# Window attention's norm roots: Newton rounds on VectorE replaced by ScalarE's Ln and Exp with one Newton round

## The reference

```python
def l2norm(t):
    return t / jnp.maximum(jnp.linalg.norm(t, axis=-1, keepdims=True), 1e-12)
...
qkv = x @ Wqkv
q, k, v = jnp.split(qkv, 3, -1)
...
q = l2norm(q) * qs
k = l2norm(k) * ksc
q = q * cos * scale + rotate_half(q) * sin * scale
k = k * cos * inv + rotate_half(k) * sin * inv
out = local_attention(q, k, v)      # softmax over 64 keys per query
```

## Time and profile before

| | |
|---|---|
| median of 3 runs | 5156.09 us (5155.09 to 5167.56) |
| the profiled execution | 5172.85 us |
| its span in the trace | 5170.8 us |
| TensorE matmul, weight load busy | 76%, 56% of the span |
| VectorE (DVE) busy | 4374.4 us, 85% |
| ScalarE (ACT) busy | 3040.4 us, 59% |
| GpSimd (POOL) busy | 2537.9 us, 49% |

### The profile page before, as it was taken

One profiled execution on the slowest core, in us unless ns is written; L12 is line 12 of the kernel. 1 busy time (PEld: TensorE's weight loads), 2 busy tenths in 40 slices (PEclk: granted clock), 3 DMA queues, 4 the chain that ended last, 5 costly groups with the idle time before them and its releaser, 6 DMA issues. The chain is left out here.

```text
span 5170.8 us, 110439 instructions
## 1 busy us (share of the span) xinstructions
PE 3934.8 (76%) x39280; PEld 2903.7 (56%) x39280; DVE 4374.4 (85%) x7725; ACT 3040.4 (59%) x4888; POOL 2537.9 (49%) x1612
## 2 busy tenths in 40 slices
PE   5777777777777777767858678777787787777787
PEld 4655655656656646625535466466465565565565
DVE  8988989979979979954335399799799899898897
ACT  4765756746747747722413477477476476575575
POOL 5645646636636636611010266366366365464562
PEclk8988999989989989986978899899899998899899
DMA  1000000000000000021030000000000000000000
GB/s 47 8 23 11 7 22 12 8 27 6 7 27 7 8 25 8 8 62 26 2 74 1 33 7 7 26 8 21 13 8 20 14 8 19 15 7 22 12 7 12
DMA packets 30608, 88.57 MB, mean 17 GB/s; under 512 B 7505, under 2 KB 13649, under 8 KB 28369
## 3 DMA queue, kind: packets, MB, share of 16 engines
q1 hardware_dynamic: 29104, 80.95, 5.9%
q10 hardware_dynamic: 1152, 3.15, 0.2%
HBM read 38.72 MB, written 1.05 MB: 8 GB/s over the span
## 5 line engine op out<-in xcount | busy, mean ns | idle before, releaser
L771 POOL TENSOR_TENSOR pool<-pool 128x512 f32<-128x512 f32 x768 | 1069.1, 1413 | 968.3 <-DVE pool L869 968.3
L776 POOL TENSOR_TENSOR pool<-pool 128x1024 f32<-128x1024 f32 x384 | 1072.8, 2794 | 168.0 <-DVE pool L880 147.2
L443 PE MATMUL psum<-squares,pool 128*128 128x128 f32 x3072 | 475.4, 304 | 420.8 <-POOL pool L776 259.9
L443 PEld LDWEIGHTS psum<-squares,pool 128*128 128x128 f32 x3072 | 368.9, 153 | 587.2 <-issue 338.1
L880 DVE TENSOR_TENSOR pool<-pool 128x1024 f32<-128x1024 f32 x384 | 678.6, 1806 | 6.8
L483 PE MATMUL psum<-wqkv_hi,xs_lo 128*128 128x512 f32 x1152 | 522.2, 453 | 200.3 <-DVE pool L849 104.6
L646 ACT COPY pool<-psum 64x512 f32<-64x512 f32 x768 | 447.1, 582 | 367.1 <-PE psum L443 361.7
L474 PE MATMUL psum<-pool 128*64 128x128 f32 x6144 | 560.7, 296 | 116.7 <-ACT pool L661 116.5
L420 PE MATMUL psum<-pool 128*128 128x128 f32 x3072 | 455.4, 309 | 130.2 <-ACT pool L646 129.8
L859 DVE TENSOR_REDUCE pool<-pool 128x16 f32<-128x1024 f32 x384 | 449.9, 1210 | 88.1 <-ACT pool L685 88.0
L420 PEld LDWEIGHTS psum<-pool 128*128 128x128 f32 x3072 | 420.4, 219 | 179.4 <-ACT pool L646 167.8
(11 more groups left out here) (165 smaller groups left out, 8247.6 us busy)
## 6 DMA issues: line engine op xcount, KB each, us to landing
pool<-pool SPq DMA_DIRECT2D x192, 128.0 KB, 2.3
pool<-in_wqkv SPq DMA_DIRECT2D x12, 1536.0 KB, 6.0
k_st<-turn_st SPq DMA_DIRECT2D x8, 1536.0 KB, 21.3
pool<-in_wo SPq DMA_DIRECT2D x12, 512.0 KB, 3.6
pool<-in_w SPq DMA_DIRECT2D x12, 341.0 KB, 3.0
pool<-in_w SPq DMA_DIRECT2D x12, 192.0 KB, 2.9
rotary<-in_rotary SPq DMA_DIRECT2D x2, 1024.0 KB, 5.4
pool<-in_scale SPq DMA_DIRECT2D x12, 128.0 KB, 6.2
```

The source lines that it names most:

```text
L443: last = pe.transpose(bank(7 - p % 2)[:, P * j:P * j + P], rot[:, p // 2, 2 * c:2 * c + 2, :], ident)
L771: last = g.tensor_tensor(rot[:, q, :, hd * r:hd * r + hd], qn[:, q, :, hd * (1 - r):hd * (2 - r)], tab, ALU.mult)
L776: g.tensor_tensor(rot[:, q], rot[:, q], by_cos[:, q], ALU.add).then_inc(rot_ready, 1)
```

## The change

A tile `least` of 128x32 is set to 1e-24 once. VectorE's `rsqrt` for the norms goes. In its place VectorE takes the maximum of the sums of squares and `least` into `held`; ScalarE, behind the softmax exponent of U-2 and ahead of `take`, computes `logs = Ln(held)` and `root = Exp(-0.5 logs)`; VectorE executes all softmax pieces of U-2 in a row, waits for `root_ready` and does one Newton round of three operations into `norm`. The other users of `rsqrt` (the layer norms) stay.

```diff
--- before.py
+++ after.py
@@ -45,6 +45,7 @@
         band_b = sb("band_b", [P, NT, 2 * WIN], bf16)
         ones = sb("ones", [P, P])
         mean_w = sb("mean_w", [P, P])
+        least = sb("least", [P, 2 * HEADS])
         ln_a = sb("ln_a", [P, B * NT])
         ln_s = [sb(f"ln_s{i}", [P, B * NT]) for i in range(4)]
 
@@ -64,6 +65,8 @@
         k_kept, s_ready, s_taken, p_ready = sem("k_kept"), sem("s_ready"), sem("s_taken"), sem("p_ready")
         block_ready, pt_ready = sem("block_ready"), sem("pt_ready")
         o_ready, o_out, wo_ready, y_ready = sem("o_ready"), sem("o_out"), sem("wo_ready"), sem("y_ready")
+        ss_ready, ss_held = sem("ss_ready"), sem("ss_held")
+        log_ready, root_ready = sem("log_ready"), sem("root_ready")
         norm_step, soft_step = sem("norm_step"), sem("soft_step")
 
         mu_ready, xc_ready, fsq_ready, var_ready = sem("mu_ready"), sem("xc_ready"), sem("fsq_ready"), sem("var_ready")
@@ -93,8 +96,8 @@
         counted = {
             "tensor": [qk_ready, v_ready, t_ready, s_ready, o_ready, wo_ready, mu_ready, var_ready,
                        rb_ready, w1_ready, w2_ready],
-            "scalar": [xs_ready, sq_ready, v_out, t_out, p_ready, pt_ready, o_out, fsq_ready, gel_ready],
-            "vector": [qn_ready, cos_ready, s_taken, block_ready, y_ready, norm_step, soft_step,
+            "scalar": [log_ready, root_ready, xs_ready, sq_ready, v_out, t_out, p_ready, pt_ready, o_out, fsq_ready, gel_ready],
+            "vector": [ss_ready, ss_held, qn_ready, cos_ready, s_taken, block_ready, y_ready, norm_step, soft_step,
                        xc_ready, diag_ready, xn_ready, hid_ready, x_ready, var_step, aff_step],
             "gpsimd": [lo_ready, w_hi, w_split, sin_ready, rot_ready, turn_ready, k_kept],
         }
@@ -176,6 +179,7 @@
                 v.tensor_copy(band_b[:].rearrange("p t k -> p (t k)"),
                               mask_f[:]).then_inc(set_up, 1)
                 v.memset(ones[:], 1.0)
+                v.memset(least[:], 1e-24)
                 v.memset(mean_w[:], 1.0 / D).then_inc(set_up, 1)
 
             @block.scalar
@@ -270,7 +274,7 @@
             by_cos = cut(2, HEADS, DH)
             rot = cut(2, HEADS, DH)
             ss = cut(2 * HEADS)
-            nwt = [cut(2 * HEADS) for _ in range(4)]
+            held, logs, root, newt, norm = [cut(2 * HEADS) for _ in range(5)]
             qT = cut(PAIRS, P)
 
             kT = [cut(PAIRS, 2, WIN + P) for _ in range(2)]
@@ -665,6 +669,13 @@
                             a.wait_ge(s_taken, done(U))
                             a.activation(S, S, ACT.Exp).then_inc(p_ready, 1)
 
+                        def roots(U):
+
+                            a.wait_ge(ss_held, done(U))
+                            a.activation(logs, held, ACT.Ln).then_inc(log_ready, 1)
+                            a.wait_ge(log_ready, done(U))
+                            a.activation(root, logs, ACT.Exp, scale=-0.5).then_inc(root_ready, 1)
+
                         def products(U):
 
                             a.wait_ge(o_ready, done(U))
@@ -686,6 +697,8 @@
                                                  ACT.Square).then_inc(sq_ready, 1)
                             if has(2):
                                 exponents(U0 + 4 * i + k - 2)
+                            if has(0):
+                                roots(U)
                             if has(-1):
                                 take(i, k + 1)
                             if has(3):
@@ -859,15 +872,24 @@
                                     last = v.tensor_reduce(ss[:, HEADS * q:HEADS * (q + 1)],
                                                            sq[:, INNER * q:INNER * (q + 1)].rearrange(
                                                                "p (h e) -> p h e", e=DH), AX.X, ALU.add)
-                                last.then_inc(norm_step, 1)
-                                v.wait_ge(norm_step, done(U, RSQRT + 1, 0))
-                                rsqrt(v, ss, nwt, norm_step, done(U, RSQRT + 1, 0), ALU.max, 1e-24, None, None,
-                                      between=probabilities(U - 2) if has(2) else ())
+                                last.then_inc(ss_ready, 1)
+                                v.wait_ge(ss_ready, done(U))
+                                v.tensor_tensor(held, ss, least[:], ALU.max).then_inc(ss_held, 1)
+                                if has(2):
+                                    for piece in probabilities(U - 2):
+                                        piece()
+                                v.wait_ge(root_ready, done(U))
+                                v.scalar_tensor_tensor(newt, root, -0.5, held, ALU.mult, ALU.mult).then_inc(norm_step, 1)
+                                v.wait_ge(norm_step, done(U, 3, 0))
+                                v.tensor_tensor(newt, newt, root, ALU.mult).then_inc(norm_step, 1)
+                                v.wait_ge(norm_step, done(U, 3, 1))
+                                v.scalar_tensor_tensor(norm, newt, 1.5, root, ALU.add, ALU.mult).then_inc(norm_step, 1)
+                                v.wait_ge(norm_step, done(U, 3, 2))
                                 v.wait_ge(sin_ready, done(U - 1, 2, 1))
                                 v.wait_ge(cos_ready, done(U - 1, 2, 1))
                                 for q in range(2):
                                     v.tensor_tensor(qn[:, q], bank(2 * q, 2).rearrange("p (h e) -> p h e", e=DH),
-                                                    nwt[3][:, HEADS * q:HEADS * (q + 1)].unsqueeze(2)
+                                                    norm[:, HEADS * q:HEADS * (q + 1)].unsqueeze(2)
                                                     .broadcast_to([P, HEADS, DH]), ALU.mult).then_inc(qn_ready, 1)
                                 if has(3):
                                     residual(U - 3, i, k - 3)
```

## The result

The changed kernel takes 5423.03 us in the median (5408.78 to 5431.87); beside it the kernel before took 5161.83. The ratio is 1.0484, 95% interval 1.046 to 1.0508: 4.8% slower, where 1.6% faster was forecast.

The account below looks back on a forecast made before the run. VectorE, busy 85% of the span, was taken to set the pace. 168 units x 0.42 plus 12 x 0.9 gave 82 us, so 5156 - 82 = 5074 us, with a range of 5025 to 5185.

Parts of the forecast that it names:

- VectorE's own sum: Window-attention unit, root's start to first product on VectorE: product at 212.15 instead of 212.57, 0.42 us earlier per unit.
- The stall moves: VectorE's wait for GpSimd at the root's seed isn't removed; the first softmax piece L815 takes it over.
- The table: ScalarE: two table loads per unit, 384 of 1.28 us, 493 us in all; Ln's load hidden before the maximum ends.
- rival 1: ScalarE's delay overtakes VectorE at products' copies, L420 and L837: slower, +84 to +113, some 5255 us; chance 0.15.
- Rival 2: No table switches on ScalarE, one load serving Ln and Exp: delay 1.28 smaller, 5015 to 5060 us; chance 0.12.
- Where this delay goes: Followed ScalarE's 3.18 us queue delay through TensorE's products and copies; claimed VectorE stays the bound, narrowly.
- 0.26 to spare at the residual: VectorE's L837: delayed output product L420 ends at 214.10, L837 starts at 214.39, leaving 0.26 with 0.03 of signalling.
- 0.5 to spare at the square: ScalarE's first square done by 220.3, VectorE's next reduction starts at 220.86: 0.5 us to spare.
- 8.84 is L837 to the next unit's root: VectorE's fixed stretch in the tightest link: unit no shorter than 17.43 us, gain capped at 0.68.
- rival 4: Maximum starts behind GpSimd's L776 and waits 2.24 us, ScalarE with it: +257, about 5410 us; chance 0.05.

Follow-up runs that it names:

- the roots late: Changed kernel with ScalarE's Ln and Exp moved behind the copies of the turned queries, both table loads and the maximum kept: 5080.6 us, ratio 0.9817.
- the busy run: Changed kernel with 15 more products, results unused, on TensorE in its wait for ScalarE's copies of the values: 5168.0 us, ratio 0.9979.

## Why the prediction was wrong, point by point

**VectorE's own sum was nearly right.** Where the maximum wins its race, as in the first units with pieces, the root's part needs 83.08 - 76.69 = 6.39 us against the 6.61 forecast and 7.03 before; and with ScalarE out of the way most units take 17.5 to 18.0 us (forecast 17.69) and the kernel 92 to 124 us below its own kernel before (forecast 82). "The stall moves" held too: the four products take 2.67 and 2.75 us in units 2 and 3 of the first layer, and 1.65 where the maximum has already waited. Units 0 and 1: VectorE reaches the product 2.91 us after the maximum's start in unit 0 (48.52 to 51.43; forecast 2.7) and 5.59 in unit 1 (60.19 to 65.78; forecast 6.2, before 7.08).

**The table was right.** Two loads per unit, nothing beside them, Ln's ahead of its wait, 0.23 us per activation (0.24 taken). Exp starts 0.01 us behind its load, and ScalarE idles 2.1 us in sum between the two over all 192 units. Ahead of the 384 loads it idles 6.9 us in sum. So a cost beside a load's 1.28 us, a case that rival 1's chance of 0.15 takes in, is not shown by any of them, and the slower result doesn't come from one. Rival 2's case, one table for both, was not what the changed program did (410 loads), but the run with one table has it (26 loads).

**The step that failed is "Where this delay goes".** It moved TensorE's work by ScalarE's delay at the durations of one unit that ran at the full clock: "L485 moves from 206.71 to 209.89 and the next product starts 0.23 later". The wait that this move opens was not looked at. TensorE then stands still for 4.14 us, and its granted clock falls. By stretches of the changed kernel (length, PE busy; the granted clock is the number behind the five busy times):

```profile
236.00:238.00 2.00, 0.00 (x0) 0.00 (x0) 1.93 (x5) 1.97 (x5) 0.47 (x1) 1.00 0.00 0
...
239.00:240.00 1.00, 1.00 (x9) 0.93 (x7) 0.96 (x4) 0.70 (x3) 0.00 (x0) 0.78 0.00 0
240.00:241.00 1.00, 1.00 (x3) 0.65 (x3) 0.93 (x5) 0.58 (x1) 0.00 (x0) 0.50 0.00 0
```

It still reads 1.00 while TensorE stands still, falls in the first microseconds after the work is taken up at 238.68, and is back at 1.00 from 243 on. The fall needs no wait as long as this one. The kernel before has it in the same place in 18 of 168 units, after waits of 0.93 us and more. One of them is the unit right behind that of the earlier trace rows:

```profile
224.95 0.78 PE L483 MATMUL psum<-wqkv_hi,xs_lo 128*128 128x512 f32 x1
225.00:226.00 1.00, 1.00 (x5) 0.76 (x3) 1.00 (x1) 0.65 (x2) 1.00 (x1) 0.50 0.00 0
```

There the keys' copies start only 0.38 us later behind the values' copies (4.52 against 4.14), because the second transposes had 0.98 us of waiting for GpSimd to lose; the delay of ScalarE takes that waiting away. So one unit was too few to take TensorE's durations from. The keys' copies L650 start 242.13 - 235.96 = 6.17 us after the maximum's end; the prediction had 210.13 + 0.69 - 205.72 = 5.10. **1.07 us** were missing, four times the 0.26 to spare at the residual and twice the 0.5 to spare at the square. Up to the first transposes the sum was exact (2.72 us after the maximum's end, in both); all of the 1.07 lies behind them, in TensorE's work at the lower clock. Keeping TensorE busy through the wait took the low clock out of all 168 of these places, brought this stretch to 5.05 us, and the kernel down by 255 us.

**The second failure is in "8.84 is L837 to the next unit's root" and in rival 4.** These 8.84 us held 1.07 of waiting in the cosine products (3.43 us for the two in the same unit of the kernel before, at 215.42; 2.36 in the changed kernel's unit above, at 246.20), because GpSimd's sine products were still running:

```profile
214.04 2.59 POOL L771 TENSOR_TENSOR pool<-pool 128x512 f32<-128x512 f32 x2 [5.14 <-DVE pool L869]
215.42 3.43 DVE L880 TENSOR_TENSOR pool<-pool 128x1024 f32<-128x1024 f32 x2
```

Once VectorE is late at the residual, GpSimd is done, and VectorE is faster from there to the reduction than I had counted; ScalarE is not. So the square, not the residual, becomes the last to come, and rival 4's sentence "both starts hang on the same VectorE instructions, so 0.05" was wrong: GpSimd's chain hangs on the cosine products' end, the maximum on that *or on ScalarE's square*. The first layer shows it happen, at the fifth unit:

```profile
76.69 0.19 DVE L877 TENSOR_TENSOR pool<-pool,least 128x32 f32<-128x32 f32 x1
...
93.93 0.19 DVE L877 TENSOR_TENSOR pool<-pool,least 128x32 f32<-128x32 f32 x1
...
103.88 0.28 DVE L850 TENSOR_TENSOR Y<-psum,X 64x128 f32 x1 [0.84 <-PE psum L424]
104.50 2.59 DVE L902 TENSOR_TENSOR pool<-pool 128x1024 f32<-128x1024 f32 x2
109.95 2.35 DVE L872 TENSOR_REDUCE pool<-pool 128x16 f32<-128x1024 f32 x2 [0.34 <-ACT pool L696]
112.34 2.03 DVE L877 TENSOR_TENSOR pool<-pool,least 128x32 f32<-128x32 f32 x1
```

Units 2 and 3 have the maximum at 0.19 us. In unit 3 the residual comes 0.84 late, the cosine products shrink from 3.77 to 2.59 us, and unit 4's reduction waits for ScalarE; its maximum is the first in a unit with pieces that GpSimd catches. It is unit 4 in all 12 layers, and from there to the layer's end every maximum is caught, 144 in all. Rival 4 was the right mechanism, but that its 5410 us lie so near the measured 5423 is partly luck: it counted 1.5 us in 168 units and had no low clock, and measured are 2.2 us in 132. It got a chance of 0.05, though ScalarE's delay, which rival 1 was given 0.15 for, is what makes the square late and the maximum lose. The two rivals were one case.

**The ledger in medians.** Change 5423; maximum away 5232 (-191); low clock away 5168 (-255); both away 5049 (-374, less than the sum of 446; in the busy run alone 66 of the 168 maxima already don't wait). The runs leave open why a unit goes from the 17.6 form into the 18.8 form in the middle of a layer when TensorE is busy; it needs a square some 0.05 us later, and where that comes from was not traced.

## What to carry to other kernels

- Moving work to an engine with 40% idle time costs nothing only if every queue behind it keeps its margin (here 586 us more on ScalarE came with a kernel 261 us longer). Write down the margin of each consumer (here 0.26 us) and compare it with the errors of the durations used; a margin smaller than those is a bound, not slack.
- Where a delay opens a new wait on TensorE, price the work behind that wait at the lower clock too (here L487 took 0.78 us at a granted clock of 0.50, where L483 took 0.48 at 1.00), and take durations from several units, with the granted clock beside each. The place of an added piece in its queue was worth 342 us here, the piece's own length next to nothing: put it behind what other engines wait for.
- A short operation that has to start before a long one on GpSimd was a switch here and not a cost: with L144 0.05 us ahead of L776's 2.37 us it took 0.18 us, and the maximum, 0.62 behind L789, took 1.80. Ask what starts each of the two, and whether anything else can delay only one of them.

## What the runs showed of the hardware

- After a wait of 4.14 us TensorE's granted clock fell to the lower level (0.78, 0.50, 0.50, 0.51 in the four microseconds from 239 to 243), and only when the work had resumed. From the first transposes to the output product it fell in 156 of 168 units of the change, in 18 of the kernel before, where the wait ahead is mostly 0.93 us, and in none with 15 more products in the wait. Giving TensorE useless work made the changed kernel 4.7% faster.
- Whether the maximum takes 0.19 us or 1.8 hangs on which of two operations starts first. In the units with pieces of the change and of the runs with one table, the roots late, both, and TensorE busy, 840 in all, every maximum that started ahead of GpSimd's operation (by 0.2 us at most) was short, and every one that started behind it (by 0.01 to 0.65 us) waited. In the kernel before, L144 leads by 0.03 to 0.18 us in all 168. A lost race isn't lost for good: with the roots behind the queries, the maximum after a caught one is short again; with TensorE busy, from a certain unit on all are caught to the layer's end, and VectorE idles mostly 0.5 to 0.6 us for the square.
- With one table for both Ln and Exp loaded explicitly at each layer's head, the 384 loads are gone (26 in the run, 410 in the change); without that the program loaded a table for each of the two in every unit, 1.283 us each, as measured 384 times.
